# Scores of layers 0, 2 and 3 and the performer's products over strips of 32 partitions

## What is computed

```python
# performer: per head h, random features rf (8 x 32)
q_kernel = jnp.exp(h_q + (proj_q - q_stab))          # proj_q = q @ rf
k_kernel = jnp.exp(h_k + (proj_k - k_stab))
q_prime, k_prime = nc * (q_kernel + KERNEL_EPS), nc * (k_kernel + KERNEL_EPS)
# causal: S += k' v^T, Z += k', out = (q' S) / (q' Z)
...
# layers 0 and 2
attn = softmax(einsum('bqhd,bkhd->bhqk', q, k) / sqrt(hd))
# layer 3
topk_scores, topk_indices = jax.lax.top_k(scores, 32)
```

## Time and profile before

| what | value |
|---|---|
| median of 3 runs | 2310.37 us (2308.21 to 2314.17) |
| the profiled execution | 2307.16 us, its span 2305.4 us |
| granted TensorE clock over the span | 0.958 |
| TensorE, weight loads | busy 89%, 70% of the span |
| VectorE, ScalarE, GpSimd | busy 85%, 64%, 41% |

### The profile page before, as it was taken

One profiled execution on the slowest core, in us unless ns is written; L12 is line 12 of the kernel. 1 busy time (PEld: TensorE's weight loads), 2 busy tenths in 40 slices (PEclk: granted clock), 3 DMA queues, 4 the chain that ended last, 5 costly groups with the idle time before them and its releaser, 6 DMA issues. The chain is left out here.

```text
span 2305.4 us, 41495 instructions
## 1 busy us (share of the span) xinstructions
PE 2055.2 (89%) x12569; PEld 1606.9 (70%) x12569; DVE 1951.0 (85%) x7828; ACT 1476.1 (64%) x3637; POOL 948.3 (41%) x1374
## 2 busy tenths in 40 slices
PE   5879798989999899998999899898999899888677
PEld 3556577656986578766886579775887669767466
DVE  1289797998989898998989899898989989796982
ACT  3546367776676667686577667676677766468341
POOL 3232213554164534544155443544345541443441
PEclk9878889999999999999999999999999999899798
DMA  4000101000100101001100101001010001001000
GB/s 188 1 8 1 35 7 50 1 8 29 56 4 1 35 6 53 1 2 35 42 18 1 35 2 56 4 1 35 13 47 1 1 29 56 31 1 56 1 3 3
DMA packets 29503, 55.03 MB, mean 24 GB/s; under 512 B 2914, under 2 KB 10082, under 8 KB 28642
## 3 DMA queue, kind: packets, MB, share of 16 engines
q1 hardware_dynamic: 29282, 52.37, 7.0%
HBM read 51.31 MB, written 1.05 MB: 23 GB/s over the span
## 5 line engine op out<-in xcount | busy, mean ns | idle before, releaser
L265 DVE MATCH_REPLACE8 top_work<-top_eight,top_work 128x256 f32<-128x256 f32 x1664 | 666.9, 408 | 0.0
L267 DVE MAX8 top_eight<-top_work 128x8 f32<-128x256 f32 x1664 | 616.7, 412 | 0.2
L305 POOL TENSOR_TENSOR top_p<-top_p,top_rest 128x512 f32<-128x512 f32 x192 | 244.4, 1273 | 217.4 <-ACT top_rest L298 217.4
L850 PE MATMUL bank<-workP 128*128 128x256 f32 x1024 | 278.1, 396 | 9.1 <-POOL workP L1012 4.0
L990 ACT ACTIVATE att_pP<-bank,att_tinyP 128x256 f32<-128x256 f32 x512 | 215.2, 476 | 67.2 <-DVE att_tinyP L1039 66.4
L850 PEld LDWEIGHTS bank<-workP 128*128 128x128 f32 x1024 | 181.3, 194 | 55.7 <-issue 29.9
L1039 DVE TENSOR_REDUCE att_tinyP<-bank 128x2 f32<-128x512 f32 x256 | 172.6, 679 | 24.1 <-PE bank L850 23.0
L267 DVE MAX8 top_lead<-bank 128x8 f32<-128x256 f32 x384 | 144.6, 417 | 46.4 <-PE bank L645 22.7
L298 ACT ACTIVATE top_rest<-top_work,top_nmax 128x256 f32<-128x256 f32 x384 | 173.3, 503 | 10.6 <-DVE top_work L265 10.3
L273 POOL TENSOR_SCALAR top_nmax<-top_lead 128x2 f32<-128x2 f32 x192 | 37.5, 195 | 336.9 <-DVE top_lead L267 336.6
L1012 POOL TENSOR_SCALAR workP<-workP,const 128x256 f32<-128x256 f32 x256 | 122.3, 484 | 130.3 <-PE bank L850 94.4
(11 more groups left out here) (365 smaller groups left out, 4587.8 us busy)
## 6 DMA issues: line engine op xcount, KB each, us to landing
gelu_w<-in_pack3w SPq DMA_DIRECT2D x72, 256.0 KB, 3.0
top_qk<-in_pack3w SPq DMA_DIRECT2D x72, 256.0 KB, 2.8
pack<-in_pack SPq DMA_DIRECT2D x1, 4352.0 KB, 19.7
pack<-in_pack SPq DMA_DIRECT2D x1, 2266.0 KB, 9.8
pack<-in_pack SPq DMA_DIRECT2D x1, 1028.0 KB, 8.1
mix_wb<-in_ctx SPq DMA_DIRECT2D x1, 1024.0 KB, 4.9
x_in<-in_x SPq DMA_DIRECT2D x8, 128.0 KB, 2.1
ctx_tok<-in_ctx SPq DMA_DIRECT2D x8, 128.0 KB, 2.4
```

The costliest lines, as they stand in the source:

```text
L265: ins = nc.vector.match_replace(self.work[:, u % 2, j, :], eight, src, GONE)
L267: ins = nc.vector.max(eight, src)
L305: self.k.nc.gpsimd.tensor_tensor(v, v, self.rest[:, :, :], ALU.subtract).then_inc(*self.p_ready.one())
L850: mm = self.k.nc.tensor.matmul(self.banks[u % 2][:, j * T:(j + 1) * T], self.q1[:, u % self.RING, j * P:(j + 1) * P], self.kT, start=True, ...
```

## The change

The weights and biases of queries and keys are permuted on the host (by_strip) so that head u has its 8 rows in strip u % 4 of 32 partitions, at place u // 4 within it. One masked copy of the queries (strip_rows) then serves four heads, one in each strip: PlainHeads makes four copies at the start in place of 16 in a ring, HeadsTop four in a ring of two. Each score contracts over its strip of 32 partitions alone. The performer's tiles have four heads in four strips already: its products read kf and qf directly, the copies by ScalarE are gone, and GpSimd adds 1e-4 to qf as well as to kf.

```diff
@@ -27,7 +27,7 @@
 SENT, GONE = -1.0e38, -3.0e38
 RF_SCALE = float(D) ** -0.25
 
-CONST = [("ident", 128), ("tri", 128), ("ones", 128), ("hsum", NG * 128), ("head_rows", H), ("group_rows", HG), ("group_eps", HG), ("part_rows", E16),
+CONST = [("ident", 128), ("tri", 128), ("ones", 128), ("hsum", NG * 128), ("strip_rows", HG), ("part_rows", E16),
          ("sim", E16), ("bq0", 1), ("bk0", 1), ("bq2", 1), ("bk2", 1), ("bq3", 1), ("bk3", 1)]
 PACK1 = [("rf", NG * 128), ("wq0", D), ("wk0", D), ("wv0", 128), ("gate0", E8), ("exp0", E8 * D), ("bias0", D)]
 PACK2 = [("wq1", H1 * HD1), ("wk1", H1 * HD1), ("wv1", H1 * HD1), ("wo1", 4 * D)]
@@ -430,14 +426,17 @@
         u = self.at(s, 0, 0)
         if u >= 0:
             if u == 0:
-                pe.wait_ge(*self.kf_ready.at(2))
+                pe.wait_ge(*self.kf_ready.at(3))
                 pe.wait_ge(*self.exp_ready.at(4))
-            pe.wait_ge(*self.q1_ready.at(u + 1))
+            if u == H // 2:
+                pe.wait_ge(*self.kf_ready.at(4))
             if u >= 2:
                 pe.wait_ge(*self.a_copied.at(u - 1))
-            out, kf, q1 = b[u % 2], self.kf[:, u // HG, :], self.q1[:, u % self.RING, :]
-            nc.tensor.matmul(out[:, 0:T], kf[:, 0:P], q1, start=True, stop=True)
-            nc.tensor.matmul(out[:, T:T + P], kf[:, P:T], q1[:, P:T], start=True, stop=True).then_inc(*self.a_ps.one())
+            g, a = divmod(u, HG)
+            r = slice(PAD * a, PAD * (a + 1))
+            out, kf, qf = b[u % 2], self.kf[r, g, :], self.qf[r, g, :]
+            nc.tensor.matmul(out[:, 0:T], kf[:, 0:P], qf, start=True, stop=True)
+            nc.tensor.matmul(out[:, T:T + P], kf[:, P:T], qf[:, P:T], start=True, stop=True).then_inc(*self.a_ps.one())
         u = self.at(s, 3, 0)
         if u >= 0 and u % 2 == 1:
             g, a = divmod(u - 1, HG)
@@ -471,12 +470,6 @@
                 act.wait_ge(*self.proj_ready.at(NG + 2 * half + 2))
                 nc.scalar.activation(self.qf[:, 2 * half:2 * half + 2, :], b[half][:, :], ACT.Exp,
                                      scale=RF_SCALE).then_inc(*self.exp_ready.one())
-            act.wait_ge(*self.exp_ready.at(4))
-            for u in range(2):
-                self.act_q1(act, u)
-        u = self.at(s, 0, 0)
-        if u >= 0 and u + 2 < H:
-            self.act_q1(act, u + 2)
         u = self.at(s, 1, 0)
         if u >= 0:
             act.wait_ge(*self.a_ps.at(u + 1))
@@ -488,15 +481,6 @@
             g = u // HG
             act.wait_ge(*self.pv_done.at(2 * g + 2))
             nc.scalar.activation(self.oT[:, g, :], b[2][:, (g % 2) * T:(g % 2 + 1) * T], ACT.Copy).then_inc(*self.oT_copied.one())
-
-    def act_q1(self, act, u):
-
-        if u >= self.RING:
-            act.wait_ge(*self.a_ps.at(u - self.RING + 1))
-        g, a = divmod(u, HG)
-        w = self.k.w
-        self.k.nc.scalar.activation(self.q1[:, u % self.RING, :], self.qf[:, g, :], ACT.Identity, bias=w["group_eps"][:, a:a + 1],
-                                    scale=w["group_rows"][:, a:a + 1]).then_inc(*self.q1_ready.one())
 
     def pool(self, pool, s):
         nc = self.k.nc
@@ -508,9 +492,9 @@
             nc.gpsimd.tensor_copy(self.v[:, :, :, 0:HD],
                                   self.ctx_tok[:, :, :].rearrange("p j (h d) -> p j h d", d=HD)).then_inc(*self.v_ready.one())
         if s == 2:
-            for half in range(2):
+            for half in range(4):
                 pool.wait_ge(*self.exp_ready.at(half + 1))
-                v = self.kf[:, 2 * half:2 * half + 2, :]
+                v = (self.kf, self.qf)[half // 2][:, 2 * (half % 2):2 * (half % 2) + 2, :]
                 nc.gpsimd.tensor_scalar(v, v, 1e-4, 1.0, ALU.add, ALU.mult).then_inc(*self.kf_ready.one())
         u = self.at(s, 2, 0)
         if u >= 0 and u % 2 == 1:
@@ -552,6 +536,11 @@
                                                    in1=self.x[:, :, :], op0=ALU.mult, op1=ALU.add))
             yield
             self.chain.ready(dve)
+
+
+def strip(u):
+
+    return slice(PAD * (u % NG), PAD * (u % NG + 1))
 
 
 class HeadsStart(Units):
@@ -635,15 +624,15 @@
 
     def score(self, pe, u):
 
-        pe.wait_ge(*self.q1_ready.at(u + 1))
+        pe.wait_ge(*self.q1_ready.at(u // NG + 1))
         if u == 0 and self.start is not None:
             pe.wait_ge(*self.start.proj_copied.at(3))
         self.score_banks_free(pe, u)
         if u >= self.ring:
             pe.wait_ge(*self.exp_done.at(u - self.ring + 1))
         for j in range(NT):
-            mm = self.k.nc.tensor.matmul(self.banks[u % 2][:, j * T:(j + 1) * T], self.tops.q1[:, u % 2, j * P:(j + 1) * P],
-                                         self.tops.k3, start=True, stop=True)
+            mm = self.k.nc.tensor.matmul(self.banks[u % 2][:, j * T:(j + 1) * T], self.tops.q1[strip(u), u // NG % 2, j * P:(j + 1) * P],
+                                         self.tops.k3[strip(u), :], start=True, stop=True)
         mm.then_inc(*self.scores.one())
 
     def pe(self, pe, s):
@@ -706,28 +695,28 @@
             if g == NG - 1:
                 act.wait_ge(*self.oT_copied.at(NG))
 
-    def pool_q1(self, pool, u):
-
-        if u >= 2:
-            pool.wait_ge(*self.scores.at(u - 1))
-        self.k.nc.gpsimd.tensor_scalar(self.tops.q1[:, u % 2, :], self.tops.q3, self.k.w["head_rows"][:, u:u + 1], 1.0,
+    def pool_q1(self, pool, a):
+
+        if a >= 2:
+            pool.wait_ge(*self.scores.at(NG * (a - 1)))
+        self.k.nc.gpsimd.tensor_scalar(self.tops.q1[:, a % 2, :], self.tops.q3, self.k.w["strip_rows"][:, a:a + 1], 1.0,
                                        ALU.mult, ALU.mult).then_inc(*self.q1_ready.one())
 
     def pool(self, pool, s):
         if s == 0:
             if self.start is not None:
                 pool.wait_ge(*self.start.proj_copied.at(3))
-            for u in range(2):
-                self.pool_q1(pool, u)
+            for a in range(2):
+                self.pool_q1(pool, a)
         u = self.at(s, 0, 0)
         if u >= 0:
             self.negative_max(pool, u)
         u = self.at(s, 1, 2)
         if u >= 0:
             self.keep_top(pool, u)
-        u = self.at(s, 0, 0) + 2
-        if 2 <= u < H:
-            self.pool_q1(pool, u)
+        u = self.at(s, 0, 0)
+        if u >= 0 and u % NG == NG - 1 and u // NG + 2 < HG:
+            self.pool_q1(pool, u // NG + 2)
 
     def dve(self, dve, s):
         for r in range(self.rounds):
@@ -807,7 +796,6 @@
 
 
 class PlainHeads(Units):
-    RING = 4
 
     def __init__(self, k, side, layer, x, ctxT, banks, tag, gate=None, router=None, before=None, start=None):
         self.name = f"heads{layer}"
@@ -843,12 +831,12 @@
             pe.wait_ge(*self.proj_copied.at(3))
             if self.rt is not None:
                 pe.wait_ge(*self.rt.e_ready.at(1))
-        pe.wait_ge(*self.q1_ready.at(u + 1))
+        pe.wait_ge(*self.q1_ready.at(u // NG + 1))
         if u >= 2:
             pe.wait_ge(*self.exp_done.at(u - 1))
         for j in range(NT):
-            mm = self.k.nc.tensor.matmul(self.banks[u % 2][:, j * T:(j + 1) * T], self.q1[:, u % self.RING, j * P:(j + 1) * P],
-                                         self.kT, start=True, stop=True)
+            mm = self.k.nc.tensor.matmul(self.banks[u % 2][:, j * T:(j + 1) * T], self.q1[strip(u), u // NG, j * P:(j + 1) * P],
+                                         self.kT[strip(u), :], start=True, stop=True)
         mm.then_inc(*self.scores.one())
 
     def projected(self, s):
@@ -1005,11 +993,9 @@
             act.wait_ge(*self.o_turned.at(1))
             nc.scalar.activation(self.otT[:, :], b[2][:, 0:T], ACT.Copy).then_inc(*self.otT_ready.one())
 
-    def pool_q1(self, pool, u):
-
-        if u >= self.RING:
-            pool.wait_ge(*self.scores.at(u - self.RING + 1))
-        self.k.nc.gpsimd.tensor_scalar(self.q1[:, u % self.RING, :], self.qT, self.k.w["head_rows"][:, u:u + 1], 1.0,
+    def pool_q1(self, pool, a):
+
+        self.k.nc.gpsimd.tensor_scalar(self.q1[:, a, :], self.qT, self.k.w["strip_rows"][:, a:a + 1], 1.0,
                                        ALU.mult, ALU.mult).then_inc(*self.q1_ready.one())
 
     def pool(self, pool, s):
@@ -1017,11 +1003,8 @@
             self.ln.pool(pool)
         if s == 2:
             pool.wait_ge(*self.proj_copied.at(self.order.index("q") + 1))
-            for u in range(3):
-                self.pool_q1(pool, u)
-        u = self.at(s, 0, 0) + 3
-        if 3 <= u < H:
-            self.pool_q1(pool, u)
+            for a in range(HG):
+                self.pool_q1(pool, a)
 
     def dve(self, dve, s):
         nc = self.k.nc
@@ -2734,15 +2717,14 @@
             rf[g, h, :, g, h, :] = a["L0_xattn_random_features"]
             hsum[g, h, :, g, h, :] = -0.5 * RF_SCALE
     w_qkv, b_qkv = a["L0_ffn_W_qkv"], a["L0_ffn_b_qkv"]
+    by_strip = np.arange(D).reshape(HG, NG, HD).transpose(1, 0, 2).reshape(D)
     parts = {
```

(17 more changed lines are left out.)

## The result

| | before | after |
|---|---|---|
| median | 2310.0 us (5 runs, 2308.2 to 2314.2) | 2538.9 us (5 runs, 2531.9 to 2546.5) |
| ratio | | 1.099, 95% interval 1.097 to 1.101 |
| profiled execution's span | 2305.4 us | 2530.0 us |
| granted clock over the span | 0.958 | 0.877 |

What follows compares the result with a forecast made beforehand. TensorE and VectorE were taken to share the bound, with TensorE at its limit where PlainHeads runs. Terms of 28 - 5 + 3 + 5 + 5 - 2 = 34 us on 2307.2, plus 3.2 to the median, gave 2345 us, range 2308 to 2392.

Steps and rivals of the forecast that it cites:

- the sum: Whole kernel: steady pairs 28, performer -5, first block's heads 3, other blocks 5 and 5, masks -2; 34 us slower.
- the heads' stretches: Layers 0 and 2 in a steady pair: 9.6 us more TensorE work, 55% let through, 5.3 us.
- Price of a border: TensorE around an isolated strip score: 0.34 us more, 0.17 a change of tile shape on average.
- Count: TensorE's timeline over the kernel: changes of tile shape go from 574 to 1218, 109 us of TensorE time.
- Sharing: Neighbouring scores in different strips run at once: up to 56 us over the kernel, 2 in a steady pair's performer stretch.
- Masks and copies priced at nearly nothing: Removed GpSimd masks worth 2 us through L645's wait behind L713; their new order and the performer's GpSimd add cost 0.
- First block, performer -5 us: Performer running alone: without ScalarE's copies 8 pairs of heads could give 6.4 us, 5 taken.
- ScalarE -75, GpSimd -129: Busy time: ScalarE loses 75 us of performer copies, GpSimd 129 us of masks, net of added adds.
- A: Whole kernel: 25% to 100% of the heads' 9.6 us passed on; 2324 to 2370 us, at most 2380; chance 0.75.
- B: Whole kernel: VectorE alone sets the pace and hides the changes of tile shape; 2310 us; chance 0.10.
- C: Whole kernel: 32-row strips cost under about 0.05 us a change, running side by side decides; 2283 us; chance 0.12.
- D: TensorE: every weight load of a strip score is exposed, 154 us more, 60% through; 2437 us; chance 0.03.

Runs made afterwards that it cites:

- only_perf: The kernel before with the change in the performer alone, heads of layers 0, 2 and 3 as before: 2389.2 us, ratio 1.034.
- rows64: The changed kernel with every score and performer product contracting over 64 rows, two strips, instead of 32: 2413.2 us, ratio 1.044.
- only_plain: The kernel before with the change in PlainHeads (layers 0 and 2) alone: 2478.5 us, ratio 1.076.
- only_top: The kernel before with the change in HeadsTop (layer 3) alone: 2338.6 us, ratio 1.011.
- tiny_strips: The kernel before with one 32-row, 8-column matmul ahead of each score and performer product, which stay over 128 rows: 2483.0 us, ratio 1.075.
- one_strip: The changed kernel with all scores and performer products in rows 0 to 31, so none run side by side: 2572.7 us, ratio 1.115.
- rows128: The changed kernel with every score and performer product contracting over all 128 rows: 2310.2 us, ratio 0.9999.

## Why the prediction was wrong

**The step that failed is the sum: it had no term for the granted clock.** The forecast read the clock only to compare the two rows, and took over 1.00 for every stretch that had it before. After had 622 - 194 = 428 us more at 1.2 GHz. What such a microsecond costs can be estimated in two ways. If TensorE alone sets the pace it costs half of itself, 214 us. Executions of one and the same kernel differ in their low time: in only_perf it was 352 us at a span of 2376.8 and 408 at 2400.0, 0.41 us for each. Over the 49 executions of the eleven kernels (after and the ten of the experiments), each taken against its own kernel's mean, it is 0.40 +- 0.02 (standard error), 171 us. The two profiled executions are 225 us apart, so by this estimate the clock took 171 to 214 of them and 11 to 54 us are left for what the forecast priced at 34.

Where the clock stayed at 1.00 the forecast's own terms can be seen by themselves. Layer 0's heads in the second pair of blocks, before and after (the same matmuls):

```profile
705.30:744.80 39.50, 38.54 (x241) 28.89 (x240) 36.64 (x138) 31.06 (x80) 20.77 (x36) 1.00 0.00 1
794.00:836.40 42.40, 42.10 (x240) 27.06 (x238) 36.54 (x137) 30.90 (x80) 13.63 (x20) 1.00 0.00 1
```

They lose 2.9 us. Layer 2's heads never had the full clock in after; in rows64 they lose 2.4 (32.4 against 30.0 us). Together that is 5.3 us a pair, which is what the forecast had for the heads' stretches. Over the six pairs the two windows grew by 8.0 and 10.3 us on average, at mean clocks of 0.89 and 0.79: the other 13 us of a pair go with the clock.

A rough sum from two prices of these runs, 0.12 us a border and 0.40 us for each microsecond of low time, comes near the other kernels: rows64 121 us (105 between the profiled executions), only_perf 74 (71), only_plain 157 (171), only_top 40 (31), after 249 less 15 to 20 for sharing (225). It is an estimate, and it does not tell why the clock falls.

The split for rows64: 105 us lost, 114 us more low time at 0.40 to 0.50, 46 to 57 us, and 48 to 59 left, more than the forecast's 34. Over the whole kernel its terms were thus somewhat low: the share that came through was over 55%, as tiny_strips showed (72 to 84%).

**Price of a border** (0.34 us for an isolated score, 0.17 a change): right. The timeline of after has 0.09 ahead of the score, 1.05 - 0.87 = 0.18 in it and 0.50 - 0.44 = 0.06 behind it, 0.33 us in all, at the places where it was expected; the 0.09 after that belongs to the next border. That a 32-row tile behaves like WideTop's 64-row one held for this price; it did not for the clock.

**Count** (574 to 1218): right, to the border.

**Sharing** (up to 56 us): 34 to 41 us between one_strip and after, 15 to 20 of them without the clock's part. The eight passes in 1.10 us are less than the 1.74 us that two scores of the earlier trace rows take one after the other. The Trainium skill (TensorE: Matmul & The Clock Gate, "Why this matters for your kernels") says that a matmul with K = 32 takes as long as one with K = 128 and gains only when others run at the same time. The trace agrees: passes over 32 rows start 0.22 us apart, as those over 128 do, an isolated score takes 1.05 us with its borders, and two take 1.10.

**Masks and copies priced at nearly nothing**: right. rows128 has them removed as after has and stands at 0.9999. The wait that the forecast valued at 2 us, L645 behind L713, fell from 23.4 to 10.6 us and gave nothing that can be measured.

**First block, performer -5 us**: too much, even at full clock. From the start of the random-feature projections of its queries (L428, L424 after) to the transposes of its output it took 26.2 us before (24.79 to 50.98), 23.7 in rows64 (24.77 to 48.50) and 23.8 in rows128: -2.5. The forecast took the 3.11 us between two pairs of heads from the earlier trace rows for all of them; the others of that stretch alternate between 3.11 and 2.41. In after the clock turned the gain into a loss: 32.0 us (25.01 to 56.99). Timeline of after, value products of successive pairs:

```profile
42.37 1.50 PE L450 MATMUL bank<-att_pTP,att_vP 128*32 128x256 f32 x8
46.30 1.50 PE L450 MATMUL bank<-att_pP,att_vP 128*32 128x256 f32 x8
```

3.93 us from one pair to the next, and the eight passes that took 0.84 us in the earlier trace rows take 1.50.

**ScalarE -75, GpSimd -129**: the copies went (128 instructions fewer on ScalarE), but ScalarE's busy time fell by 54 only. Added up one by one, the durations of its instructions fell by 78 us (1766.9 to 1688.7); busy time counts a moment once, and part of the copies' time was covered by neighbours that overlap them in the record. GpSimd's fell by 127.

**The rivals.** A had the mechanism of the borders and lacked the clock. B (VectorE hides it) falls with the wait of 118.1 us. C (faster) would have needed a change under 0.05 us; it was 0.15 to 0.17. D came nearest to the time, 2437, by a mechanism that isn't there: the passes of a strip score start 0.22 us apart (L634 at 516.62, 516.84 and 517.06; the four of the isolated score at 518.87 fit in 1.05 us), with their loads hidden. The rule of the Trainium skill (TensorE: Matmul & The Clock Gate, Part 3, "What overlaps and what doesn't") on which D rested is contradicted by that spacing: all four passes of that score are in one strip. No rival named the clock, although showed stretches at 0.88 and 0.50 before.

## To carry to other kernels

Before matmuls are cut to fewer rows of the array, ask whether anything runs beside them: a score that stands alone between full-array work gains nothing in time, pays some 0.3 us for its two changes of shape, and here its likes brought the clock down for all that TensorE did near them. Read the granted clock of each stretch beside its busy time; where TensorE is the bound, a forecast needs a term of about 0.4 to 0.5 us for each microsecond at the lower level. A masked copy on an idle engine is a cheap way to keep a contraction full.

## What was not expected of the hardware

- The same list of matmuls in the same order spent 199, 308 and 622 us at 1.2 GHz when the changed scores contracted over 128, 64 and 32 rows. TensorE was busy 89, 90 and 91% of these spans.
- The fall isn't even, and the windows shown above are of one pair. Over the six steady pairs layer 0's heads had 0.89 in two and 1.00 in four at 64 rows, and 1.00 in one and 0.86 to 0.89 in five at 32; layer 2's had 0.90 in two and 1.00 in four at 64 rows, and 0.72 to 0.86 at 32. What sets this apart was not found.
- Single stretches can go against the whole. Heads alone, 29 us before, took 38.0 us at 0.73 over 64 rows (60.9 to 98.9) and 34.7 at 0.80 over 32. In the pair shown, layer 2's heads had 0.86 in one_strip (615.0 to 652.2, 37.2 us) and 0.72 in after; over the six pairs the two kernels are alike (40.4 and 40.3 us).
- 888 changes of tile shape left the clock where it was (0.961).
- Adding full-array passes raised the clock in one stretch and shortened it (51.6 to 49.0 us), and did nothing for it in another that was already at the lower level.
